# Self-attention on one core: row sums by additions on POOL, work items in two halves around the maxima, a halved item's result taken one slot later

## The chip, the cores and the metric

The kernel runs on one core of one Trainium2 chip. The metric is the device time of one execution in microseconds (us). The core has five engines with a queue each: TensorE (PE, matmuls), VectorE (DVE), ScalarE (ACT), GpSimd (POOL) and SyncE (SP, which issues DMAs). An instruction starts when those before it on its engine are done and its semaphore waits are met.

## The reference

A decoder layer: gated recurrence, cross-attention, then self-attention with a mixture of experts; the change lies in the self-attention alone. For B=4 batches of T=512 tokens, H=512, 16 heads of 32, in float32:

```python
q = (h @ wq + bq).reshape(B, S, N_HEADS, HEAD_DIM)
...
q, k = _rope(q, k)
...
scores = jnp.einsum('bqhd,bkhd->bhqk', q, k) * HEAD_DIM ** (-0.5)
causal = jnp.tril(jnp.ones((S, S), bool))
scores = jnp.where(causal[None, None], scores, jnp.finfo(scores.dtype).min)
attn = jax.nn.softmax(scores, axis=-1)
ctx = jnp.einsum('bhqk,bkhd->bqhd', attn, v).reshape(B, S, N_HEADS * HEAD_DIM)
x = x + ctx @ wo
h = _rms(x, w_ln2).reshape(B * S, H)
```

## The kernel before

`self_attention` runs 16 **steps** n = 0 to 15. Step n is batch b = n // 4 and group c = n % 4 of four heads. Each step has four **slots** kt = 0 to 3, one for each block of 128 keys; under the causal mask slot kt covers the last 512 - 128 kt queries. One slot on PE is, in order:

- `scores(n, kt)` (L1727, L1731, L1733): the scores of the four heads, keys on partitions, into four PSUM banks, with the row maximum taken off (`negm`, L1731) and the mask added.
- the slot's **early items** (`put`): projections and transposes of other steps that fill PE while ACT works, each into bank 6 or 7 in turn. An A item is the query or key projection of step n+2, a V item 128 rows of values, an O item 128 rows of the output projection (12 matmuls through L134 each). An H item transposes the normed input of the next batch (L1675), G, R and L items belong to the experts. H items are **late items**: they come behind the slot.
- `maxima(n + 1, 3 - kt)` (L1717, L1719): scores of the next step with queries on partitions, for its row maxima, into the same four PSUM banks. It waits for Exp, which empties them.
- `weighted(n, kt)`: probabilities times values (L1745), and probabilities times a block of ones (L1747), which are the sums for the softmax; each is four matmuls in float32, added up over the four slots in banks 4 and 5.

After slot 3 PE puts the T item (L1711), which turns the maxima; ACT writes them to `negm` (L1501), and the next step's scores begin.

ACT does in each slot Exp (L1529) from the four banks into `pT[:, kt % 2]`, then takes the items' results out of banks 6 and 7 (`take`; A: L1495 to `qk`, V: L1497). DVE does in each slot `maximum(n + 1, 3 - kt)` (L1616), a reduction from the four banks which frees them for the next slot's scores, then for an A item the shuffle (L1581) and the product with the sine (L1583) that the rotation needs, for an O item the two residual additions (L1593, L1595). At the end of the step it takes the reciprocal of the sums (L1648) and scales the output (L1650). POOL rotates step n+2's query and key during step n (`rotate`: L1427 waits for ACT's `qk`, L1430 for DVE's sine product), sometimes takes an inverse root (L1420), and behind the step's last scores splits the rotated pair into a high and a low part (L1444, L1447).

The `Steps` class writes out by hand which item stands in which slot. A items stand in slots 0 and 2 where c = 0 and in slots 0 and 1 elsewhere; V items of the own batch in slots 1 and 3 where c = 0, of the next batch in slots 2 and 3 where c = 3; O items of the batch before in slot 3 where c = 1 (two) and in slots 2 and 3 where c = 2. Batch 0 has no O items, the last batch no H items.

## Time and profile before

| | us |
|---|---|
| median of 3 runs | 2553.0 (2551.19 to 2557.34) |
| the profiled execution, its own time | 2558.96 |
| its span, first to last instruction | 2557.2 |
| TensorE busy in the span | 2399.1 (94%) |
| VectorE busy | 1353.7 (53%) |
| ScalarE busy | 1348.8 (53%) |
| GpSimd busy | 919.3 (36%) |

The 16 steps lie between 1407 and 1821 us of the span. In rows of a time line the first column is the start, the second how long the merged instructions took from the first start to the last end; then engine, line, operation, names (written<-read), shapes and count. In brackets stands how long the engine sat idle before the row, and what ended the idle time. Matmuls overlap, so that the time PE spends on a row is best read as the distance from its start to the start of the next. A float32 matmul with 32 rows of output shows as two records.

### The profile page before, as it was taken

The numbers are of one execution on the slowest core, as the hardware profiler recorded it, in microseconds if no ns is written. First come the engines' busy times: TensorE is split into PE (matmuls) and PEld (weight loads), VectorE is DVE, ScalarE is ACT, GpSimd is POOL, SyncE is SP. The second block draws the span as 40 slices with busy tenths as digits, with TensorE's granted clock in tenths as the row PEclk, the third lists the DMA queues.
The fourth block names the chain that finished last, engine by engine and source line by source line (L and its number), as shares of the span: only waits on it lengthen the run. The fifth ranks groups of instructions, "written<-read, shape, count | busy, mean of one in ns | idle before, by whom it ended". The sixth has DMA issues, their size and how long they took to land. (4 is left out here: it accounts for less than half of the span.)

```text
span 2557.2 us, 39125 instructions
## 1 busy us (share of the span) xinstructions
PE 2399.1 (94%) x15376; PEld 1547.3 (61%) x15376; DVE 1353.7 (53%) x2114; ACT 1348.8 (53%) x1708; POOL 919.3 (36%) x608
## 2 busy tenths in 40 slices
PE   7997899989999999999997999998899999999997
PEld 5885644444444444444333555555578899999885
DVE  5566634434344434434413556555475577776785
ACT  4221467666767777767895434433332266665221
POOL 1223744655355544655202333332034012121320
PEclk8998999999999999999999999999899999999999
DMA  5002675576547653775653300001045267775430
GB/s 181 17 1 72 192 224 126 126 197 170 141 116 209 168 153 93 180 203 143 173 124 104 111 1 1 18 18 53 34 140 170 90 228 233 243 244 186 152 113 37
DMA packets 206983, 331.46 MB, mean 130 GB/s; under 512 B 71312, under 2 KB 125840, under 8 KB 206608
## 3 DMA queue, kind: packets, MB, share of 16 engines
q1 hardware_dynamic: 188304, 252.80, 34.9%
q0 software_dynamic: 16336, 72.23, 8.6%
q10 hardware_dynamic: 2160, 3.93, 0.6%
q8 instruction: 122, 2.00, 0.3%
q14 instruction: 61, 0.50, 0.1%
HBM read 241.53 MB, written 99.42 MB: 133 GB/s over the span
## 5 line engine op out<-in xcount | busy, mean ns | idle before, releaser
L938 ACT ACTIVATE A_c_prob<-c_psum 128x1024 f32<-128x1024 f32 x832 | 787.1, 1029 | 285.9 <-PE c_psum L1188 273.0
L864 POOL TENSOR_TENSOR c_rr<-c_ms,c_half 128x32 f32<-128x32 f32 (+1 forms) x72 | 372.6, 5177 | 426.4 <-DVE c_ms L955 424.8
L1197 PE MATMUL c_psum<-A_c_prob,c_vq 128*17 128x512 f32 x3328 | 417.0, 601 | 8.3 <-DVE c_oT L1092 8.1
L134 PE MATMUL c_psum<-R_c_w,S_c_c 128*128 128x512 f32 x1248 | 313.9, 401 | 0.7 <-DVE S_c_c L966 0.5
L1188 PE MATMUL c_psum<-c_qq,c_kq 64*128 64x512 f32 x1664 | 288.3, 438 | 26.6 <-DMA c_vq<-vd 14.5
L134 PEld LDWEIGHTS c_psum<-R_c_w,S_c_c 128*128 128x128 f32 x1248 | 227.9, 189 | 121.9 <-issue 40.7
L1188 PEld LDWEIGHTS c_psum<-c_qq,c_kq 64*128 64x128 f32 x1664 | 136.9, 186 | 175.6 <-ACT A_c_prob L938 92.6
L995 DVE COPY Q_c_unit<-c_psum 128x256 f32<-128x256 f32 x89 | 37.8, 425 | 333.6 <-PE c_psum L134 333.6
L2363 PE MATMUL m_psum<-A_m_dn_hi,A_m_a 128*128 128x512 f32 (+1 forms) x628 | 204.4, 394 | 2.4 <-DVE A_m_a L2160 2.4
L134 PE MATMUL m_psum<-R_m_t,m_up_hi 128*128 128x256 f32 (+1 forms) x1104 | 200.0, 283 | 0.0
L1616 DVE TENSOR_REDUCE s_topx<-s_psum 128x4 f32<-128x2048 f32 (+1 forms) x64 | 95.5, 1493 | 172.2 <-PE s_psum L1719 167.5
L1197 PEld LDWEIGHTS c_psum<-A_c_prob,c_vq 128*17 128x17 f32 x3328 | 68.8, 96 | 189.1 <-issue 165.3
L134 PEld LDWEIGHTS m_psum<-R_m_t,m_up_hi 128*128 128x128 f32 (+1 forms) x1104 | 165.8, 179 | 2.1
L2099 ACT ACTIVATE A_m_a<-Q_m_work 128x256 fp32r<-128x256 f32 (+2 forms) x113 | 56.7, 502 | 201.4 <-DVE Q_m_work L2155 171.1
L134 PE MATMUL m_psum<-R_m_t,m_up_lo 128*128 128x256 f32 (+1 forms) x552 | 154.7, 280 | 0.0
L1529 ACT ACTIVATE A_s_pT<-s_psum 128x2048 f32<-128x2048 f32 (+1 forms) x64 | 79.5, 1242 | 125.1 <-PE s_psum L1733 124.7
L2363 PEld LDWEIGHTS m_psum<-A_m_dn_hi,A_m_a 128*128 128x128 f32 (+1 forms) x628 | 117.8, 188 | 29.0 <-DVE A_m_a L2160 3.0
L2363 PE MATMUL m_psum<-Q_m_dn_lo,A_m_a 128*128 128x512 f32 (+1 forms) x314 | 123.1, 392 | 0.0
L2092 ACT ACTIVATE Q_m_work<-m_psum 128x256 f32<-128x256 f32 (+2 forms) x113 | 51.9, 459 | 134.4 <-PE m_psum L134 133.0
L857 POOL TENSOR_TENSOR S_c_c<-Q_c_raw,S_c_c 128x512 fp32r<-128x512 f32 x89 | 118.8, 1335 | 7.1
L134 PE MATMUL m_psum<-R_g_hi,m_up_hi 128*128 128x512 f32 x264 | 105.6, 400 | 3.6 <-DVE m_up_lo L2137 3.6
L2137 DVE TENSOR_TENSOR m_up_lo<-S_up_raw,m_up_hi 128x1408 fp32r<-128x1408 f32 (+2 forms) x70 | 102.6, 1471 | 5.7 <-ACT m_up_hi L2053 3.1
(298 smaller groups left out, 4282.1 us busy)
## 6 DMA issues: line engine op xcount, KB each, us to landing
c_kq<-kd SPq DMA_DIRECT2D x248, 208.0 KB, 6.1
kd<-S_c_t SPq DMA_DIRECT2D x96, 256.0 KB
Q_c_raw<-in_ctxT SPq DMA_DIRECT2D x89, 256.0 KB
qd<-A_c_q SPq DMA_DIRECT2D x64, 256.0 KB
c_qq<-qd SPq DMA_DIRECT2D x64, 256.0 KB, 3.1
vd<-A_c_vt SPq DMA_DIRECT2D x104, 136.0 KB, 4.1
c_vq<-vd SPq DMA_DIRECT2D x31, 442.0 KB, 9.1
R_m_hs<-slots SPq DMA_DIRECT2D x23, 512.0 KB
```

Of the source, the lines that this page charges most:

```text
L134: mm = pe.matmul(out, a(c), b(c), start=first and i == 0, stop=last and i == len(terms) - 1)
L857: pool.tensor_tensor(c_lo[:, job % 2], c_raw[:, n % CB], c_hi[:, job % 2], ALU.subtract).then_inc(s_clo, 1)
L864: pool.tensor_tensor(rr[:, unit % RB, 0:n], ms[:, unit % RB, 0:n], half[:, 0:n], ALU.pow).then_inc(s_r, 1)
L938: act.activation(prob[:, t % PB, 2 * (u % 2):2 * (u % 2) + 2, :], score_banks[u % 3], ACT.Exp, scale=XD ** -0.5).then_inc(s_ex, 1)
L1188: mm = pe.matmul(score_banks[u % 3][:, s, :], kq[rows, q % 2, u % 2, kt * P:(kt + 1) * P], qq[rows, q % 2, u % 2, :], start=True, stop=True)
L1197: mm = pe.matmul(o_bank[32 * j:32 * j + VW, :], vq[:, q % 2, kt, j, :], prob[:, t % PB, j, :], start=kt == 0, stop=kt == CT - 1)
L1529: act.activation(pT[:, kt % 2, :, 0:L], psum[:, 0:HPC, 0:L], ACT.Exp, scale=SCALE).then_inc(s_ex, 1)
L1616: dve.reduce_max(topx[:, t, ::SD], psum[:, 0:HPC, 0:(t + 1) * P], AX_X).then_inc(s_top, 1)
L2092: act.activation(sig[0:rows, 0:width], gu_bank[n % 2][0][0:rows, 0:width], ACT.Sigmoid).then_inc(s_sig, 1)
L2099: act.activation(a_hi[0:rows, p % 2, i, 0:width], act_f[0:rows, 0:width], ACT.Copy).then_inc(s_ahi, 1)
L2137: dve.tensor_tensor(up_lo[:, w % 2, j, :, 0:cols(w)], up_raw[:, j, :, 0:cols(w)], up_hi[:, w % 2, j, :, 0:cols(w)], ALU.subtract).then_inc ...
L2363: mm = pe.matmul(y_bank[t], a[0:rows, p % 2, i, ts], w[0:rows, i, :], start=k == 0, stop=k == 3 * len(x.chunks) - 1)
```

## The change

The sums over keys are no longer matmuls in each slot. Exp of slot 0 writes `p_even`, those of slots 1 to 3 write `p_odd`; POOL adds each of the latter onto the matching part of `p_even` (`add`, L1460 of the changed kernel), and one set of four matmuls per step (`sums`, L1795) multiplies the added probabilities by the ones. The T item stands behind `sums` on PE. POOL's order in a step is now add 1, rotate query, add 2, rotate key, add 3, halves. Exp of slots 2 and 3 waits for the add before, since it overwrites `p_odd`. A slot's last A, V or O item is issued in two halves of six matmuls, one ahead of `maxima`, one behind `weighted` (`halved`); V item kt in slot kt stays whole. Where a halved item is held (`held`: slots 0 to 2 without late items), ACT and DVE take its result in the next slot (`taken`).

```diff
+    def halved(self, n, kt):
+        return [item for item in self.early[n][kt][-1:] if n + 1 < self.N and item.kind in "AVO" and (item.kind, item.i) != ("V", kt)]
+    def held(self, n, kt):
+        return self.halved(n, kt) if 0 <= kt < TT - 1 and not self.late[n][kt] else []
+    def taken(self, n, kt):
+        late = self.held(n, kt)
+        return self.held(n, kt - 1) + [item for item in self.early[n][kt] if item not in late]
...
-        pT = A.tile("s_pT", 0, 2, HPC, T)
+        p_even, p_odd = (A.tile(f"s_p{i}", i * HPC * T, HPC, T) for i in range(2))
+        pT = [p_even, p_odd[:, :, 0:T - P], p_odd[:, :, 0:T - 2 * P], p_odd[:, :, 0:P]]
...
+            def add(n, kt):
+                pool.wait_ge(s_pv, n * TT + 1)
+                pool.wait_ge(s_ex, n * TT + kt + 1)
+                if kt > 1:
+                    pool.wait_ge(s_add, n * (TT - 1) + kt - 1)
+                pool.tensor_tensor(pT[0][:, :, kt * P:T], pT[0][:, :, kt * P:T], pT[kt], ALU.add).then_inc(s_add, 1)
...
+            for n in range(STEPS):
+                b, c = divmod(n, KC)
+                more = n + 2 < STEPS
+                add(n, 1)
+                if c == KC - 1 and b:
+                    inverse_root("O", b - 1)
+                if more:
+                    rotate(n + 2, 0)
+                add(n, 2)
+                if more:
+                    rotate(n + 2, 1)
+                add(n, 3)
+                if c == 0 and b + 1 < B:
+                    inverse_root("H", b + 1)
+                if more:
+                    halves(n + 2)
...
-                    if n * TT + kt >= 2:
-                        act.wait_ge(s_pv, n * TT + kt - 1)
+                    if kt == 0 and n:
+                        act.wait_ge(s_sum, n)
...
+                    if kt >= 2:
+                        act.wait_ge(s_pv, n * TT + kt)
+                        act.wait_ge(s_add, n * (TT - 1) + kt - 1)
...
-                    for item in line.early[n][kt]:
+                    for item in line.taken(n, kt):
                         take(item)
...
-                dve.wait_ge(s_pv, n * TT + TT)
+                dve.wait_ge(s_sum, n + 1)
...
-                for j in range(HPC):
-                    mm = pe.matmul(sum_bank[rows[j], qs], ones[:], pT[:, kt % 2, j, 0:L], start=kt == 0, stop=True, skip_group_check=True)
-                mm.then_inc(s_pv, 1)
+            def sums(n):
+                pe.wait_ge(s_add, (n + 1) * (TT - 1))
+                for j in range(HPC):
+                    mm = pe.matmul(sum_bank[rows[j], :], ones[:], pT[0][:, j, :], start=True, stop=True)
+                mm.then_inc(s_sum, 1)
...
+                    for item in halved:
+                        put(item, 0)
                     if more:
                         if kt == 0:
                             pe.wait_ge(s_hi, 2 * n + 2)
                         pe.wait_ge(s_ex, n * TT + kt + 1)
                         maxima(n + 1, TT - 1 - kt)
                     weighted(n, kt)
+                    for item in halved:
+                        put(item, 1)
                     for item in line.late[n][kt]:
                         put(item)
+                sums(n)
                 if more:
                     put(line.turn[n + 1])
```

DVE's queue through step 4 (c = 0), from the reciprocal of step 3 to the last reduction, first before (`s_topx` rows are the maxima of step 5, the `s_turned` pairs the sine products of the two A items):

```order
L1648 RECIPROCAL s_a<-s_psum 128x512
L1650 TENSOR_TENSOR s_a<-s_psum,s_a 128x512
L1616 TENSOR_REDUCE s_topx<-s_psum 128x4
L1620 SCALAR_TENSOR_TENSOR A_s_a_15499<-s_a,s_bv,A_s_a_15498 128x512
L1581 STREAM_SHUFFLE s_turned<-s_qk 128x512
L1583 TENSOR_TENSOR s_turned<-s_turned,s_sin 128x512
L1616 TENSOR_REDUCE s_topx<-s_psum 128x4 x2
L1581 STREAM_SHUFFLE s_turned<-s_qk 128x512
L1583 TENSOR_TENSOR s_turned<-s_turned,s_sin 128x512
L1570 TENSOR_SCALAR s_ms<-s_ss 128x4
L1616 TENSOR_REDUCE s_topx<-s_psum 128x4
```

And now, the same stretch to its end, with the reciprocal of the step behind it:

```order
L1684 RECIPROCAL s_a<-s_psum 128x512
L1686 TENSOR_TENSOR s_a<-s_psum,s_a 128x512
L1652 TENSOR_REDUCE s_topx<-s_psum 128x4
L1656 SCALAR_TENSOR_TENSOR A_s_a_15500<-s_a,s_bv,A_s_a_15499 128x512
L1652 TENSOR_REDUCE s_topx<-s_psum 128x4
L1617 STREAM_SHUFFLE s_turned<-s_qk 128x512
L1619 TENSOR_TENSOR s_turned<-s_turned,s_sin 128x512
L1652 TENSOR_REDUCE s_topx<-s_psum 128x4
L1606 TENSOR_SCALAR s_ms<-s_ss 128x4
L1652 TENSOR_REDUCE s_topx<-s_psum 128x4
L1617 STREAM_SHUFFLE s_turned<-s_qk 128x512
L1619 TENSOR_TENSOR s_turned<-s_turned,s_sin 128x512
```

The first pair moved from slot 0 to slot 1, the second from ahead of the step's last reduction to behind it.

POOL's queue of one step where c = 2, before (`Q_s_qk` rows are the halves):

```order
L1427 TENSOR_TENSOR s_rot<-s_qk,s_cos 128x512
L1430 TENSOR_TENSOR s_rot<-s_rot,s_turned 128x512
L1427 TENSOR_TENSOR s_rot<-s_qk,s_cos 128x512
L1430 TENSOR_TENSOR s_rot<-s_rot,s_turned 128x512
L1444 CAST Q_s_qk_1776<-s_rot 128x512 x2
L1447 TENSOR_TENSOR Q_s_qk_1777<-s_rot,Q_s_qk_1776 128x512 x2
```

And now (`A_s_p_15497` is `p_even`, `A_s_p_15498` is `p_odd`):

```order
L1460 TENSOR_TENSOR A_s_p_15497<-A_s_p_15497,A_s_p_15498 128x4x384
L1440 TENSOR_TENSOR s_rot<-s_qk,s_cos 128x512
L1443 TENSOR_TENSOR s_rot<-s_rot,s_turned 128x512
L1460 TENSOR_TENSOR A_s_p_15497<-A_s_p_15497,A_s_p_15498 128x4x256
L1440 TENSOR_TENSOR s_rot<-s_qk,s_cos 128x512
L1443 TENSOR_TENSOR s_rot<-s_rot,s_turned 128x512
L1460 TENSOR_TENSOR A_s_p_15497<-A_s_p_15497,A_s_p_15498 128x4x128
L1450 CAST Q_s_qk_1776<-s_rot 128x512 x2
L1453 TENSOR_TENSOR Q_s_qk_1777<-s_rot,Q_s_qk_1776 128x512 x2
```

Three additions came in, and the last, on which `sums` waits, stands behind both rotations.

PE's queue in slot 3 of step 4 from the last mask matmuls of the item-free part on, before:

```order
L1717 MATMUL s_psum<-Q_s_qk_1776 128x128 x4
L1719 MATMUL s_psum<-s_neg,ident 128x128 x4
L1745 MATMUL s_psum<-A_s_pT,s_v 32x128 x4
L1747 MATMUL s_psum<-A_s_pT,s_ones 32x128 x4
L1711 MATMUL s_psum<-ident,s_topx 128x128 x4
```

And now:

```order
L1761 MATMUL s_psum<-Q_s_qk_1776 128x128 x4
L1763 MATMUL s_psum<-s_neg,ident 128x128 x4
L1789 MATMUL s_psum<-A_s_p_15498,s_v 32x128 x4
L1795 MATMUL s_psum<-A_s_p_15497,s_ones 32x512 x4
L1754 MATMUL s_psum<-ident,s_topx 128x128 x4
```

The sums of the whole step, 512 wide, stand where those of slot 3, 128 wide, stood; the ones of slots 0 to 2 are gone.

## Rows read from the trace of the kernel before

**Rows 1.** Busy time of each engine in two stretches, from Exp 0 to Exp 0

```profile
core 0: us, PE busy (x) PEld busy (x) DVE busy (x) ACT busy (x) POOL busy (x), PEclk, DMA share, GB/s
1526.24:1552.17 25.93, 23.85 (x233) 15.25 (x233) 16.15 (x19) 13.45 (x18) 11.44 (x11) 1.00 0.00 1
```

**Rows 2.** Time line of PE in step 4 (c = 0)

```profile
1505.10 0.51 PE L1727 MATMUL s_psum<-Q_s_qk 32*128 32x512 f32 x4
...
1506.51 0.71 PE L134 MATMUL s_psum<-S_s_h,R_s_hi 128*128 128x512 f32 x2
...
1509.45 0.51 PE L1717 MATMUL s_psum<-Q_s_qk 32*128 32x512 f32 x4
...
1511.11 1.04 PE L1747 MATMUL s_psum<-A_s_pT,s_ones 128*32 128x512 f32 x8
1512.68 0.45 PE L1727 MATMUL s_psum<-Q_s_qk 32*128 32x384 f32 x4 [0.53 <-DVE s_topx L1616]
...
1513.79 0.48 PE L134 MATMUL s_psum<-R_s_hi,S_s_h 128*128 128x512 f32 x1
...
1516.72 0.45 PE L1717 MATMUL s_psum<-Q_s_qk 32*128 32x384 f32 x4
...
1518.10 0.83 PE L1747 MATMUL s_psum<-A_s_pT,s_ones 128*32 128x384 f32 x8
1519.35 0.39 PE L1727 MATMUL s_psum<-Q_s_qk 32*128 32x256 f32 x4 [0.42 <-DVE s_topx L1616]
...
1525.19 0.33 PE L1727 MATMUL s_psum<-Q_s_qk 32*128 32x128 f32 x4 [0.32 <-DVE s_topx L1616]
...
1530.48 0.63 PE L1711 MATMUL s_psum<-ident,s_topx 128*128 128x128 f32 x4
```

**Rows 3.** Time line of ACT, step 4 and the start of step 5

```profile
1506.74 1.88 ACT L1529 ACTIVATE A_s_pT<-s_psum 128x2048 f32<-128x2048 f32 x1 [0.93 <-PE s_psum L1733]
...
1514.02 1.46 ACT L1529 ACTIVATE A_s_pT<-s_psum 128x1536 f32<-128x1536 f32 x1 [1.80 <-PE s_psum L1733]
...
1532.67 1.88 ACT L1529 ACTIVATE A_s_pT<-s_psum 128x2048 f32<-128x2048 f32 x1 [0.93 <-PE s_psum L1733]
```

**Rows 4.** Time line of DVE in step 4

```profile
1510.33 2.29 DVE L1616 TENSOR_REDUCE s_topx<-s_psum 128x4 f32<-128x2048 f32 x1 [1.94 <-PE s_psum L1719]
...
1525.07 0.73 DVE L1581 STREAM_SHUFFLE s_turned<-s_qk 128x512 f32<-128x512 f32 x1
1525.83 0.69 DVE L1583 TENSOR_TENSOR s_turned<-s_turned,s_sin 128x512 f32<-128x512 f32 x1
...
1529.64 0.69 DVE L1616 TENSOR_REDUCE s_topx<-s_psum 128x4 f32<-128x512 f32 x1 [3.04 <-PE s_psum L1719]
```

**Rows 5.** Groups of POOL instructions, each shape apart: busy us, mean ns

```profile
L1427 POOL TENSOR_TENSOR s_rot<-s_qk,s_cos 128x512 f32<-128x512 f32 x30 | 38.4, 1281 | 137.5 <-ACT s_qk L1495 137.5
...
L883 POOL CAST R_s_hi<-A_c_stage 128x2048 fp32r<-128x2048 f32 x2 | 3.8, 1900 | 12.8 <-DMA A_c_stage<-in_wq 12.1 <-DMA A_c_stage<-in_wv 0.6
```

**Rows 6.** Time line of POOL ahead of step 0

```profile
1405.06 4.58 POOL L1447 TENSOR_TENSOR Q_s_qk<-s_rot,Q_s_qk 128x512 fp32r<-128x512 f32 x2
```

**Rows 7.** Time line of ACT: Exp 0 of steps 2 and 3

```profile
1458.59 1.89 ACT L1529 ACTIVATE A_s_pT<-s_psum 128x2048 f32<-128x2048 f32 x1 [0.92 <-PE s_psum L1733]
...
1480.82 1.88 ACT L1529 ACTIVATE A_s_pT<-s_psum 128x2048 f32<-128x2048 f32 x1 [0.92 <-PE s_psum L1733]
```

**Rows 8.** Time line of PE: the T item at the end of step 5

```profile
1560.31 0.66 PE L1711 MATMUL s_psum<-ident,s_topx 128*128 128x128 f32 x4 [1.53 <-DVE X L1595]
```

**Rows 9.** Time line of ACT in step 15

```profile
1811.03 1.45 ACT L1529 ACTIVATE A_s_pT<-s_psum 128x1536 f32<-128x1536 f32 x1
...
1815.07 1.03 ACT L1529 ACTIVATE A_s_pT<-s_psum 128x1024 f32<-128x1024 f32 x1 [1.44 <-PE s_psum L1733]
```

**Rows 10.** Busy time by stretch behind step 15, columns as in group 1

```profile
1824.00:1828.00 4.00, 1.08 (x3) 0.92 (x4) 3.18 (x5) 1.49 (x3) 0.00 (x0) 0.78 0.00 0
1828.00:1832.00 4.00, 4.00 (x11) 3.13 (x10) 1.41 (x3) 0.00 (x0) 0.00 (x0) 0.50 0.00 0
```

**Rows 11.** Time line of PE: the first scores of step 15

```profile
1803.25 0.80 PE L1727 MATMUL s_psum<-Q_s_qk 32*128 32x512 f32 x4
```

More of the change, by code:

```diff
@@ L1359, in self_attention @@
         rr = m.sb("rr", [P, TT])
-        unused = pT[:, 1, :, T - P:T]
+        unused = p_odd[:, :, T - P:T]
         psum, bank = m.banks()
@@ L1370, in self_attention @@
         s_vs, s_qb, s_tc, s_turned, s_sin, s_rot, s_hi, s_lo = m.sem("vs", "qb", "tc", "turned", "sin", "rot", "hi", "lo")
-        s_max, s_top, s_ng, s_st, s_ex, s_pv = m.sem("max", "top", "ng", "st", "ex", "pv")
+        s_max, s_top, s_ng, s_st, s_ex, s_pv, s_add, s_sum = m.sem("max", "top", "ng", "st", "ex", "pv", "add", "sum")
         s_rec, s_a, s_ahi, s_alo, s_x1, s_x = m.sem("rec", "a", "ahi", "alo", "x1", "x")
@@ L1430, in rotate, with halves @@
                 pool.tensor_tensor(rot[:, i], rot[:, i], turned[:, i], ALU.add).then_inc(s_rot, 1)
-            pool.wait_ge(s_ld, 80)
-            for n in range(1, STEPS):
-                for i in range(2):
-                    rotate(n, i)
-                if n % KC == 2 and n // KC + 1 < B:
-                    inverse_root("H", n // KC + 1)
-                if n % KC == 1 and n // KC >= 2:
-                    inverse_root("O", n // KC - 2)
+            def halves(n):
                 if n >= 2:
@@ L1447, in _ @@
                     pool.tensor_tensor(qk_lo[:, n % 2, i], rot[:, i], qk_hi[:, n % 2, i], ALU.subtract).then_inc(s_lo, 1)
-            for b in (B - 2, B - 1):
-                inverse_root("O", b)
+            def add(n, kt):
[4 more added lines that the diff above has]
+                pool.tensor_tensor(pT[0][:, :, kt * P:T], pT[0][:, :, kt * P:T], pT[kt], ALU.add).then_inc(s_add, 1)
+            pool.wait_ge(s_ld, 80)
+            for i in range(2):
+                rotate(1, i)
+            halves(1)
+            for n in range(STEPS):
[14 more added lines that the diff above has]
+                    halves(n + 2)
+            inverse_root("O", B - 1)
         @block.scalar
@@ L1638, in _ @@
                         low_output(n - 1)
-                    for item in line.early[n][kt] + line.late[n][kt]:
+                    for item in line.taken(n, kt) + line.late[n][kt]:
                         take(item)
@@ L1662, in _, with put, product @@
             rows = [slice(SD * j, SD * j + SD) for j in range(HPC)]
-            def put(item):
+            def put(item, part=None):
                 dst = bank_of(item)
-                if item.old:
+                if item.old and part != 1:
                     pe.wait_ge(emptied[item.old.kind], item.old.nth)
                 i, n = item.i, item.n
+                k0, k1 = {None: (0, KC), 0: (0, KC // 2), 1: (KC // 2, KC)}[part]
+                def product(lhs_hi, lhs_lo, rhs_hi, rhs_lo):
+                    return product3(pe, dst, lambda k: lhs_hi(k0 + k), lambda k: lhs_lo(k0 + k), lambda k: rhs_hi(k0 + k), lambda k: rhs_lo(k0 + k),
+                                    k1 - k0, first=k0 == 0, last=k1 == KC)
                 b, c = divmod(n, KC)
@@ L1679, in put @@
                         pe.wait_ge(s_hlo, b * KC)
-                    mm = product3(pe, dst, lambda k: w_hi[i][:, k, fs], lambda k: w_lo[i][:, k, fs], *h, KC)
+                    mm = product(lambda k: w_hi[i][:, k, fs], lambda k: w_lo[i][:, k, fs], *h)
                 if item.kind == "V":
@@ L1683, in put @@
                         pe.wait_ge(s_hlo, n * KC)
-                    mm = product3(pe, dst, lambda k: h_hi[:, k, ts], lambda k: h_lo[:, k, ts], lambda k: w_hi[2][:, k, :], lambda k: w_lo[2][:, k, :], KC)
+                    mm = product(lambda k: h_hi[:, k, ts], lambda k: h_lo[:, k, ts], lambda k: w_hi[2][:, k, :], lambda k: w_lo[2][:, k, :])
                 if item.kind == "O":
@@ L1688, in put @@
                     at = lambda k: (n * KC + k) % RING
-                    mm = product3(pe, dst, lambda k: a_hi[:, at(k), ts], lambda k: a_lo[:, at(k), ts], lambda k: w_hi[3][:, k, :], lambda k: w_lo[3][:, k, :], KC)
+                    mm = product(lambda k: a_hi[:, at(k), ts], lambda k: a_lo[:, at(k), ts], lambda k: w_hi[3][:, k, :], lambda k: w_lo[3][:, k, :])
                 if item.kind == "G":
@@ L1711, in put @@
                         mm = pe.transpose(dst[:, t * P:(t + 1) * P], topx[:, t, :], ident[:])
-                mm.then_inc(s_put, 1)
+                if part != 0:
+                    mm.then_inc(s_put, 1)
             def maxima(n, t):
@@ L1766, in _ @@
                     scores(n, kt)
-                    for item in line.early[n][kt]:
+                    early = line.early[n][kt]
+                    halved = line.halved(n, kt)
+                    for item in early[:len(early) - len(halved)]:
                         put(item)
+                    for item in halved:
+                        put(item, 0)
                     if more:
```

9 lines of the change are left out of this document (5 added, 4 removed).

## The prediction, made before the changed kernel ran

> **What bounds the kernel now.** I first looked at busy time over one step. Of 25.93 us PE is busy 23.85 and POOL 11.44, and the granted clock is 1.00, the 2.4 GHz level [rows 1]. So PE sets the pace here and POOL has 14 us free. The time line of PE shows how a slot is spent. The reader is to see two things in it. First, PE hardly waits: only 0.53, 0.42 and 0.32 us ahead of the scores of slots 1 to 3, each time for DVE's reduction [rows 2]. Second, behind PE's own work runs a second chain through the four PSUM banks that is nearly as long: scores, Exp, maxima, reduction, next scores.
>
> For slot 0 that chain is 1.64 us from scores to Exp (1505.10 to 1506.74), Exp 1.88, 0.05 to hand over, 0.88 from maxima to reduction (1509.45 to 1510.33), reduction 2.29, 0.06 to hand over: 6.80 us. The slot takes 7.58 (1505.10 to 1512.68), because the item of 2.94 us keeps PE beyond Exp's end [rows 2 to 4].
>
> **What the change takes out, by slot.** Issue times are distances between starts. The sums of slot 0 cost PE about 0.89 us, those of slot 1 0.67; by width I take 0.45 and 0.25 for slots 2 and 3. That is 2.26 per step, of which 0.89 is paid once again in `sums`. Halving the item moves 1.47 us behind `weighted`, where it covers the reduction.
> - Slot 0: PE would need 3.57 to Exp's end, 1.66 for maxima and weighted (1509.45 to 1511.11) and 1.47 for the second half, 6.70; the bank chain is 6.80. From 7.58 to 6.80: 0.78 gained.
> - Slot 1: scores to Exp is 1.34 (1512.68 to 1514.02), Exp 1.46, so maxima begin at 2.85; then 1.38 (1516.72 to 1518.10) and 1.47 give 5.70, from 6.67: 0.97 gained.
> - Slot 2 in the same way: about 4.94 from 5.84, 0.90 gained.
>
> Slots 0 to 2 thus give 2.65 us wherever each has a halved item. Exp loses its cover in slot 0 (0.65 us of PE waiting), and this is already in these numbers.
>
> **What the change adds: the chain on POOL.** `sums`, and behind it T and the next scores, wait for add 3, and add 3 is behind add 1, two rotations and add 2. No row shows an addition of this shape. Product with the cosine, two inputs in SBUF, is 1.281 us for 512 elements [rows 5]. The adds cover 1536, 1024 and 512 elements: by proportion 3.84, 2.56 and 1.28, together 7.7 us. From below I bound them by the one-input CAST, 1.900 for 2048 elements [rows 5]: 2.85 us in all. From above by the pair of subtractions that ran while DVE read two SBUF inputs: 4.58 us instead of 2.56, 1.8 times as much [rows 6], 13.8 us in all. I take 7.7, since the nearest row has the same operation and type.
>
> The Trainium skill, GPSIMD Engine Reference, section 3.1, gives 4497 ns for a float32 addition of 2048 elements. Estimated from that page the adds would be 3.4, 2.2 and 1.1 us, 0.9 less per step, and the sum below would come out some 6 us lower, at about 2552.
>
> Counted from the start of scores 1: Exp 1 ends at 2.80, add 1 at 6.7. Each rotation is 2.57 (two instructions of 1.28), so the rest is 2.57 + 2.56 + 2.57 + 1.28, and add 3 ends at 15.7. Exp 2 and Exp 3 wait for the adds before them by 0.2 us at most, which is hidden under the first half of the item. PE reaches the place of `sums` at 5.70 + 4.94 + 4.57 = 15.2 where slot 3 has a halved item (0.81 scores, 2 x 1.47 item, 0.59 maxima, 0.23 weighted). Then 0.95 for `sums`, 0.56 for T, 6.80 for slot 0: the new period is 15.7 + 8.3 = 24.0. Now by kind of step:
>
> - Steps 3, 6, 10 (c = 3 of batch 0, c = 2 with O items): 24.0 from 25.93 (distance of Exp 0 to Exp 0, as 1506.74 to 1532.67 [rows 3]): -1.9 each, **-5.8**.
> - Steps 7 and 11: an inverse root of 1.0 us stands in POOL's chain: -0.9 each, **-1.8**.
> - Step 2 has no items in slots 2 and 3 and took 22.23 [rows 7]. It becomes 24.0, since POOL's chain does not care: **+1.7**. Step 1 likewise **+0.5**.
> - Steps 5, 9, 13: slot 3 holds two O items, so add 3 is long done when `sums` comes. T ended its wait for DVE's O item at 1560.31 [rows 8]; the halved item lets DVE begin 1.5 us sooner. With 0.78 in slot 0, 0.6 in slots 1 and 2 (H items fill there) and 1.2 in slot 3: -2.6 each, **-7.8**. Step 14: 2.26 - 0.95, **-1.3**.
> - Steps 0, 4, 8, 12 (c = 0). Here the second A item is in slot 2, is held, and DVE's shuffle and sine product now stand behind the step's last reduction. The whole V item of slot 3 is still ahead of those maxima, so the reduction ends 5.14 us after scores 3 (1525.19 to 1529.64, and 0.69) [rows 2, 4]. Then shuffle 0.73 and product 0.69 [rows 4], POOL's rotation sum 1.29, add 3 1.28, `sums` 0.95 and hand-overs 0.15: T starts at 10.2 instead of 5.29 (1525.19 to 1530.48 [rows 2]). That is 4.9 lost against 2.65 gained: +2.25 each, **+9.0**.
> - Step 15 has no cover: Exp 2 waits for add 1, at 1811.03 + 1.45 + 3.94 = 1816.4 instead of 1815.07 [rows 9]; step 15's last add and full-width sums lie bare on the way to the tail. Add 2 makes up for part: **+1.9**.
>
> Sum: -3.8 us. So the work saved is paid back by the wait for add 3.
>
> **And the clock.** In the four steps with c = 0 PE stands idle from the end of weighted, about 4.9 after scores 3, to 9.3: 4.4 us, more than any wait inside the steps today. The trace shows what followed a long wait: in 1824 to 1828 PE was busy 1.08 us of 4, and in the 4 us after it the granted clock was 0.50, the 1.2 GHz level [rows 10]. After the 1.53 us wait [rows 8] it stayed at 1.00. Scores at a lowered clock took 0.80 against 0.51 for the same four matmuls [rows 2, 11]. Sums, T and scores together are 0.89 + 0.56 + 1.41 = 2.86 us on the path, and between 0.57 and 1.0 times as much again is 1.6 to 2.9; I take 2.3, four times: **+9.2**. The Trainium skill, TensorE: Matmul & The Clock Gate, part 1, says that the engine is throttled to half its clock when it idles and is released by activity; by that rule the trace agrees (0.50 behind the wait), and it speaks against this change.
>
> Sum with the clock: +5.4 us. The profiled execution's own time is 2558.96 (span 2557.2, 1.8 around it) and would become 2564.4; it is 6 above the median of the runs, 2553.0, which would become **2558**.
>
> **Edits costed at nothing.** The later take of A and V results: banks 6 and 7 alternate, and the item before is taken in the slot after, ahead of its bank's next use. DVE's reciprocal (3.36 of work behind `sums` instead of behind slot 3) has to be ready by weighted 0, about 5.5 us after T starts; it is, with under 1 us to spare. If that cover is gone it is a wait in weighted 0 of what is missing. The halves of step n+2 end 5 us ahead of their use. No DMA is moved.
>
> **The rivals.**
> - The clock holds (free of the +9.2): 2553 - 4 = **2549**. For it: 1.5 us waits left it at 1.00 [rows 8]. Against: the wait here is three times as long.
> - POOL is slower than by proportion (the other side: slower). Place: add 1 to add 3, in front of `sums`. DVE's sine products read two SBUF inputs inside that chain, and such an overlap stretched a pair from 2.56 to 4.58 [rows 6]; four pieces per partition may cost too. At 25% more on the adds the seven steps 1, 2, 3, 6, 7, 10, 11 lose 1.9 each, the four with c = 0 0.3, the tail 1.5: 16 us, with the clock **2574**, without it 2565. It decides (beyond 0.3%, 7.7 us) from 5% on if the clock falls.
> - POOL is much cheaper, towards the CAST, and the clock holds: then PE's own work bounds. Steps 3, 6, 10 gain 0.5 more, 7 and 11 1.5, 1 and 2 about 2, c = 0 0.5: 10 us more than -4, **2539**.
>
> **How the numbers follow.** Forecast 2558: 0.42. Clock holds, 2549: 0.25. POOL slower: 0.20. POOL cheaper: 0.13. 0.3% is 7.7 us, about what a measurement of this kernel tells from no change. Of the forecast's spread (2553 to 2563) a quarter is beyond +7.7, of the second case a sixth beyond -7.7. Slower: 0.20 + 0.11 = 0.31. Faster: 0.13 + 0.04 = 0.17. Same: 0.52. Leaving out the far half of each outer case gives 2544 to 2571.
>
> **What would show it.** Adds of 3.8, 2.6 and 1.3 us; POOL busy about 19 of a 24 us step; PE idle about 4.4 us ahead of `sums` in steps 0, 4, 8 and 12 and 0.5 to 3 in the others but 5, 9, 13; a period of 28.2 (more with the clock) for c = 0 and 24.0 for steps 3, 6, 10; the clock below 1.00 behind the waits of c = 0. I am wrong if the adds are off by more than 10%, if the clock holds, or if DVE's reciprocal turns up as a wait.

## The result, and the profile after

The changed kernel took 2567.8 us (median of 8 runs, 2564.4 to 2578.6); the kernel before took 2558.3 in its 8 runs of the same measurement (2551.2 to 2562.5). The ratio is 1.0049, with a 95% interval from 1.0035 to 1.0064: slower by 0.49%, 12.5 us of 2558 (9 to 16). A second measurement of the same kernel, below, gave 1.0045. The forecast was +5.4 us (2558), with a chance of 0.52 for a change within 0.3%, 0.31 for slower, and a range of 2544 to 2571. The sign came out as foreseen and the time lies in the slow part of the range, but the loss is 2.3 times the size forecast, and the case that came was not the one I held likeliest.

The profiled execution of the changed kernel took 2578.62 us (span 2576.9), 11 above the median of its runs; the one of before was also above its median. So I compare distances between Exps here, not spans. Busy time over step 4 (c = 0), in three stretches of 4 us around its end, and over step 6 (c = 2); columns as in [rows 1]:

```profile
core 0: us, PE busy (x) PEld busy (x) DVE busy (x) ACT busy (x) POOL busy (x), PEclk, DMA share, GB/s
1517.26:1548.56 31.30, 26.24 (x205) 15.59 (x205) 16.50 (x16) 11.19 (x19) 17.52 (x13) 0.90 0.00 1
1540.00:1544.00 4.00, 1.01 (x8) 0.20 (x8) 0.32 (x1) 0.00 (x0) 3.54 (x4) 0.78 0.00 0
1544.00:1548.00 4.00, 4.00 (x30) 1.98 (x23) 3.00 (x1) 0.60 (x1) 3.52 (x4) 0.50 0.00 0
1548.00:1552.00 4.00, 3.66 (x26) 2.21 (x26) 1.59 (x3) 3.44 (x4) 0.00 (x0) 0.87 0.02 4
1576.98:1601.75 24.77, 24.06 (x205) 14.46 (x205) 16.75 (x18) 8.78 (x13) 16.30 (x11) 1.00 0.01 2
```

Step 4 took 31.30 us where it took 25.93 [rows 3]; step 6, which also took 25.93, took 24.77. In step 4 the granted clock is 0.90 on the whole, and 0.50, the 1.2 GHz level, from 1544 to 1548.

The stretch of [rows 1] is as long as step 4, but it doesn't run from Exp 0 to Exp 0: those are at 1506.74 and 1532.67 [rows 3]. Over step 4 itself, before the change, the row is

```profile
1506.74:1532.67 25.93, 24.42 (x229) 15.60 (x229) 13.20 (x15) 11.41 (x19) 9.73 (x9) 1.00 0.01 2
```

so POOL was busy 9.73 us of it, and not 11.44. In step 6 it was 8.81.

The time line of PE at the end of step 4 shows the wait itself. Here the sums of the step, then T, then scores 0 of step 5 follow:

```profile
1538.40 0.42 PE L1789 MATMUL s_psum<-A_s_p,s_v 128*32 128x128 f32 x8 [0.18 <-ACT s_v L1530]
1542.99 1.93 PE L1795 MATMUL s_psum<-A_s_p,s_ones 128*32 128x512 f32 x8 [4.16 <-POOL A_s_p L1460]
1544.86 1.12 PE L1754 MATMUL s_psum<-ident,s_topx 128*128 128x128 f32 x4
1545.90 0.80 PE L1771 MATMUL s_psum<-Q_s_qk 32*128 32x512 f32 x4
```

PE stands idle for 4.16 us ahead of `sums`, released by POOL's addition (L1460). Behind the wait T takes 1.12 us instead of 0.66 and the first scores 0.80 instead of 0.51 [rows 2, 8]. What POOL waited for is on the time lines of DVE and POOL:

```profile
1538.26 0.69 DVE L1652 TENSOR_REDUCE s_topx<-s_psum 128x4 f32<-128x512 f32 x1 [3.74 <-PE s_psum L1763]
...
1538.87 0.72 DVE L1617 STREAM_SHUFFLE s_turned<-s_qk 128x512 f32<-128x512 f32 x1
1539.62 0.69 DVE L1619 TENSOR_TENSOR s_turned<-s_turned,s_sin 128x512 f32<-128x512 f32 x1
```

```profile
1536.11 1.29 POOL L1440 TENSOR_TENSOR s_rot<-s_qk,s_cos 128x512 f32<-128x512 f32 x1 [1.62 <-ACT s_qk L1528]
1540.46 1.26 POOL L1443 TENSOR_TENSOR s_rot<-s_rot,s_turned 128x512 f32<-128x512 f32 x1 [3.06 <-DVE s_turned L1619]
1541.68 1.26 POOL L1460 TENSOR_TENSOR A_s_p<-A_s_p,A_s_p 128x512 f32<-128x512 f32 x1
```

The chain reads: last reduction, shuffle, product with the sine, POOL's rotation sum, add 3, `sums`. POOL was idle for 3.06 us in the middle of it. It isn't short of time; its queue holds add 3 behind a rotation that waits for DVE.

The additions by shape, and the product with the cosine, from 1407 to 1850 [rows 5]:

```profile
L1460 POOL TENSOR_TENSOR A_s_p<-A_s_p,A_s_p 128x1536 f32<-128x1536 f32 x16 | 55.7, 3483 | 152.1 <-ACT A_s_p L1565 152.1
L1440 POOL TENSOR_TENSOR s_rot<-s_qk,s_cos 128x512 f32<-128x512 f32 x28 | 44.5, 1591 | 6.6 <-ACT s_qk L1528 6.6
...
L1460 POOL TENSOR_TENSOR A_s_p<-A_s_p,A_s_p 128x1024 f32<-128x1024 f32 x16 | 38.0, 2375 | 1.6 <-ACT A_s_p L1565 1.6
...
L1460 POOL TENSOR_TENSOR A_s_p<-A_s_p,A_s_p 128x512 f32<-128x512 f32 x16 | 20.4, 1277 | 6.0 <-ACT A_s_p L1565 6.0
```

The additions cost 3.48, 2.38 and 1.28 us, the first two less than I had taken. The product with the cosine rose from 1281 ns [rows 5] to 1591 on average.

By kind of step, the distance from Exp 0 to Exp 0, against before. The steps measured are those of a second profiled execution of the changed kernel (r1_changed below), in which the clock held in step 1:

| steps | forecast, all together | measured |
|---|---|---|
| 0, 4, 8, 12 (c = 0) | +18.2 (9.0 wait, 9.2 clock) | +17.6 |
| 3, 6, 10 | -5.8 | -3.5 |
| 7, 11 | -1.8 | -0.5 |
| 5, 9, 13 | -7.8 | -3.2 |
| 1 and 2 | +2.2 | +5.3 |
| 14 | -1.3 | -2.3 |
| sum of the 15 steps | +3.7 | +13.4 |

The first profiled execution gives +18.8 for the sum: its step 1 took 26.91 us where this one's took 24.55, and each of its steps 0, 4, 8 about 1 us more.

### The profile page after: what moved, and what is told of

The parts are those of the page before. It is cut to its first block and busy times, and to the rows that moved or that the text cites. A ratio compares the mean times of both kernels' runs of the same rounds, so it can differ in the third digit from the quotient of the medians.

```text
span 2576.9 us, 38446 instructions
## 1 busy us (share of the span) xinstructions
PE 2404.2 (93%) x14992; PEld 1536.7 (60%) x14992; DVE 1369.6 (53%) x2114; ACT 1346.2 (52%) x1708; POOL 1040.9 (40%) x656
## 5 line engine op out<-in xcount | busy, mean ns | idle before, releaser
L1460 POOL TENSOR_TENSOR A_s_p<-A_s_p,A_s_p 128x1536 f32<-128x1536 f32 (+2 forms) x48 | 114.2, 2378 | 159.8 <-ACT A_s_p L1565 159.8
L1565 ACT ACTIVATE A_s_p<-s_psum 128x2048 f32<-128x2048 f32 (+1 forms) x64 | 79.4, 1240 | 153.1 <-PE s_psum L1777 136.3
L2067 POOL DMA_INDIRECT S_up_raw<-in_up,m_up_row x46 | 44.4, 964 | 164.1 <-DVE m_up_lo L2192 163.8
```

Of the source, the lines that this page charges most:

```text
L1460: pool.tensor_tensor(pT[0][:, :, kt * P:T], pT[0][:, :, kt * P:T], pT[kt], ALU.add).then_inc(s_add, 1)
L1565: act.activation(pT[kt], psum[:, 0:HPC, 0:L], ACT.Exp, scale=SCALE).then_inc(s_ex, 1)
```

## The experiments

Theory A was that the loss sits in the four steps with c = 0 and comes from add 3's place behind the late rotation. Theory B was that it is POOL's extra work as such. Theory C was that the gain of halving is small, whoever makes the sums. All ratios are to the kernel before in runs on the same chip.

**Add 3 ahead of the second rotation.**

```
                 add(n, 2)
+                add(n, 3)
                 if more:
                     rotate(n + 2, 1)
-                add(n, 3)
```

> POOL's order is add 1, rotate query, add 2, add 3, rotate key. Theory A (the loss is the wait of the sums for add 3, long only because add 3 stands behind the key's rotation): in steps with c = 0 add 3 ends about 3 us after the last scores start, ahead of PE, so the 4.2 us wait and the lowered clock behind it go; about 6.8 us less in each of steps 0, 4, 8 and 12, and 3 to 4 less in steps 1 and 2: 30 us below the changed kernel, near 2537 to 2545, 0.5 to 0.8% faster than before. Theory B (the additions load POOL too much wherever they stand, or PE loses by the halved items): the order moves work only, under 8 us less, near 2560 to 2567.

Measured: 2539.9 us, ratio 0.9944 (0.9931 to 0.9958), 14 us faster than before and, by the two ratios, about 27 faster than the changed kernel. Nothing but the order of one queue differs. The c = 0 steps take 24.57 instead of 30.3, which is 23 of the 27 us. The first fence is from the list of PE's waits in the changed kernel (us in total, times, longest); the second has Exp 0 of steps 4, 5 and 6 on ACT with add 3 first:

```profile
PE s_psum L1795 <- POOL A_s_p L1460: 22.9, 9, 4.2
```

```profile
1501.62 1.88 ACT L1565 ACTIVATE A_s_p<-s_psum 128x2048 f32<-128x2048 f32 x1 [0.93 <-PE s_psum L1777]
1526.19 1.88 ACT L1565 ACTIVATE A_s_p<-s_psum 128x2048 f32<-128x2048 f32 x1 [0.93 <-PE s_psum L1777]
1554.68 1.88 ACT L1565 ACTIVATE A_s_p<-s_psum 128x2048 f32<-128x2048 f32 x1 [0.93 <-PE s_psum L1777]
```

With add 3 first, `sums` waited 1.4 us in all, in two places, instead of 22.9 in nine; from Exp 0 of step 4 to that of step 5 it is 24.57 us. POOL does as much work as before the edit (1039.2 us busy against 1040.9). Theory B had under 8 us less, and falls by this.

**The second A item of c = 0 taken in its own slot.** This removes the same wait from the other side: DVE gets its shuffle and product done before the last reduction, and POOL's order stays as in the changed kernel.

```
     def held(self, n, kt):
-        return self.halved(n, kt) if 0 <= kt < TT - 1 and not self.late[n][kt] else []
+        return self.halved(n, kt) if 0 <= kt < TT - 1 and not self.late[n][kt] and (n % KC, kt) != (0, 2) else []
```

> The changed kernel, but the second A item of the steps with c = 0 is taken by ACT and DVE in its own slot 2 (still in two halves); POOL's order stays. Theory A (the wait of c = 0 comes from the sine product behind the step's last reduction): the product is ready 4 us earlier, add 3 ends about when PE is done, c = 0 falls from 31.3 to 25 or 26 us, 20 us below the changed kernel: 2542 to 2550. Theory B (it is add 3 behind any second rotation, held or not): under 6 us gained.

Measured: 2549.0 us, 0.9978 (0.9967 to 0.9988). The c = 0 steps take 25.2 us, and the waits ahead of `sums` come to 7.9 us in all instead of 22.9. So four takes, each moved by one slot, turn a kernel slower by 0.45% into one faster by 0.22%. This and the edit before confirm theory A twice, by independent edits.

**Additions left out.** POOL only signals where each addition stood, and `sums` multiplies the cosine table, so the softmax is divided by sums that are not its own; everything else is computed.

```
-                pool.tensor_tensor(pT[0][:, :, kt * P:T], pT[0][:, :, kt * P:T], pT[kt], ALU.add).then_inc(s_add, 1)
+                pool.sem_inc(s_add, 1)
```

> Leaves the additions out: POOL only signals, and the sums' four matmuls read a constant tile, so that the softmax is divided by wrong sums. Everything else as in the changed kernel, POOL's order with its waits too. Theory A (the place in POOL's queue, not POOL's load): the signal of add 3 still comes behind the key's rotation, so c = 0 keeps 29 to 30 us; the other steps lose what the additions cost them, steps 1 and 2 about 2 to 4 us each; 8 to 12 us below the changed kernel. Theory B (POOL's load): c = 0 falls to 25 us as well, 35 us below.

Measured: 2550.5 us, 0.9985 (0.9976 to 0.9994). Even with 120 us of POOL's work gone (920.2 busy against 1040.4), the c = 0 steps still take 28.1 to 28.4 us, 2.2 to 2.5 more than in the kernel before. That is under the 29 to 30 I expected, and the kernel came out 14.8 us below the changed one on the same chip, not 8 to 12. PE still waits ahead of its sums (here L1796), for a signal that stands behind the rotation in POOL's queue:

```profile
1530.60 1.07 PE L1796 MATMUL s_psum<-s_cos,s_ones 128*32 128x512 f32 x8 [1.87 <-POOLq L1460]
```

```profile
1530.36 1.27 POOL L1443 TENSOR_TENSOR s_rot<-s_rot,s_turned 128x512 f32<-128x512 f32 x1 [3.06 <-DVE s_turned L1619]
```

The rows show one thing more. `sums` began at 1530.60, 0.24 us into the rotation's last instruction and 1.03 ahead of its end (1531.63), and so it did in all four c = 0 steps: the bare signal waited for the instruction ahead of it to start, not to end. So this kernel leaves out more than the additions, and its wait is too short. As an estimate, a signal at the rotation's end would make it 1.87 + 1.03 = 2.9 us, and add 3 itself (1.26) brings that to the 4.16 measured. Most of the wait is made by the place in the queue; the additions lengthen it. A kernel with free additions in this order would be slower than one with real additions in the better order (2550.5 against 2539.9, on two chips whose kernel before took 2553.8 and 2553.5).

**Sums on PE, halves and late takes kept.** All of the change but the additions: PE makes the sums of each slot again, POOL has its old order.

```
-        pT = [p_even, p_odd[:, :, 0:T - P], p_odd[:, :, 0:T - 2 * P], p_odd[:, :, 0:P]]
+        pT = A.tile("s_pT", 0, 2, HPC, T)
...
+            for n in range(1, STEPS):
+                for i in range(2):
+                    rotate(n, i)
```

> Items in halves and results taken late as in the changed kernel, but the sums as matmuls in each slot and POOL's queue as before the change. Theory A: with the additions gone nothing waits for POOL; the halves gain 0.3 to 0.4 us in slots 1 and 2 less 0.2 us that each halved item costs PE in hand-overs: within 5 us of before. Theory B (the halves themselves cost the time): as slow as the changed kernel, 2565 or more.

Measured: 2566.7 us, 1.0049 (1.0035 to 1.0062), outside what I expected. The c = 0 steps took 25.97 and the steps 3, 6, 10 25.7 to 26.5, no gain. By its number it is what theory B gave, so the run has to be read step by step. The list of PE's waits tells why the undisturbed steps gain nothing: those for the maxima (scores behind DVE's reduction) fell from 16.6 us to 1.1, but those for Exp (maxima behind ACT) rose from 8.3 to 19.7, and new ones came up for POOL's halves (3.7) and for DVE's scaled output (3.2, from 0.3). With PE's own sums in place a halved item only trades one wait for the others. Most of the loss (9.0 of 13.7 us over the steps) lies in two steps and has, as I read the trace, another source, a fault of my kernel rather than of the idea. In steps 7 and 11 (31.17 and 29.72 us) the late take delays a rotation, and the inverse root is behind it in POOL's old order. ACT's normalise stands ahead of Exp 3 and begins 0.11 us behind the root's end (the trace names no releaser for it):

```profile
1607.98 1.28 POOL L1442 TENSOR_TENSOR s_rot<-s_rot,s_turned 128x512 f32<-128x512 f32 x1 [1.91 <-DVE s_turned L1595]
1609.22 1.02 POOL L1432 TENSOR_TENSOR s_rr<-s_ms,s_half 128x4 f32<-128x4 f32 x1
```

```profile
1610.35 1.33 ACT L1485 ACTIVATE A_s_xs<-A_s_xs,s_rr 128x512 f32<-128x512 f32 x2 [5.62 <-issue]
```

It is the same fault of order as that of add 3, with another operation behind the late rotation. The changed kernel has the root right behind add 1 and doesn't suffer from it. No run with the root moved tests this reading. The run therefore tells what halves do in the undisturbed steps (nothing), and not what the part costs as a whole.

**Items whole, additions on POOL**, once in the changed kernel's order and once with add 3 first.

```
     def halved(self, n, kt):
-        return [item for item in self.early[n][kt][-1:] if n + 1 < self.N and item.kind in "AVO" and (item.kind, item.i) != ("V", kt)]
+        return []
```

> Sums by additions on POOL as in the changed kernel, but each item whole and taken in its own slot. Slots 0 to 2 then go back to 7.6, 6.7 and 5.8 us, since the sums that left PE lay under DVE's reduction. Theory A: A1 of c = 0 is taken in slot 2, so the sine product is ready in slot 3 and the wait of 4.2 us shrinks to 1 to 2; each step pays sums (0.95) and a wait for add 3 in the steps without O or V items at its end: 5 to 15 us slower than before. Theory B: the wait for add 3 stays as long as in the changed kernel and nothing is gained in the slots: 30 us slower than before.

> Items whole and taken at once, add 3 ahead of the key's rotation: neither halves nor any long wait. Slots stay at 7.6, 6.7, 5.8 us, each step pays the sums at its end, 0.95 less the 0.25 of slot 3's: about 0.3 us slower per full step, 1 to 2 in steps 1 and 2: 0.1 to 0.4% slower than before, 2555 to 2562. If additions gain by themselves, it is faster than before.

Measured: 2562.7 us, 1.0040 (1.0026 to 1.0053), and 2561.0, 1.0026 (1.0017 to 1.0036). Both lie where I expected them. With whole items nothing is held, so add 3 is seldom late (`sums` waits 2.9 us in three places in the first, 1.1 in two in the second), and its place matters little. The full steps take 26.2 to 26.5 us, 0.3 to 0.6 more than before. The waits for the maxima in the first of these kernels, and below them those of the kernel before:

```profile
PE s_psum L1771 <- DVE s_topx L1652: 41.5, 38, 1.4
```

```profile
PE s_psum L1727 <- DVE s_topx L1616: 16.6, 38, 0.6
```

The same 38 places, and 25 us more. The sums of slots 0 to 2 are gone from PE, but they had stood under DVE's reduction, so that PE now waits out most of what it saved, and pays 1.0 us for the sums of the step on top. Halves alone gain nothing, additions alone lose, and both together with add 3 first gain 1.1 to 1.4 us in each full step (24.57 for c = 0, 24.7 for steps 3, 6, 10, 24.8 for steps 7 and 11). Each part needs the other: one takes PE's work out from under the reduction, and the other puts the item there.

**The wait filled with PE work**, to price the clock: in c = 0 steps 16 matmuls into a bank that is free go ahead of `sums`; their results are not used.

```
+                if n % KC == 0:
+                    item = line.turn[n + 1]
+                    pe.wait_ge(emptied[item.old.kind], item.old.nth)
+                    for k in range(16):
+                        pe.matmul(bank_of(item), w_hi[0][:, k % KC, 0:P], h_hi[:, k % KC, :], start=True, stop=True)
```

> The changed kernel, and in the four steps with c = 0 PE runs 16 matmuls of 512 columns into the bank of the T item, which overwrites them, ahead of the sums (extra work, no result changed). Theory A, its clock part: the wait stays about as long in sum (3.7 us of matmuls, then the rest of 4.2) but the clock stays at 1.00, so sums, T and scores take 2.9 us and not 5: 2 to 2.5 us less per step, 8 to 10 us below the changed kernel. Theory B (the clock costs nothing here): no gain, or up to 1 us more per step where the matmuls outlast the wait.

Measured: 2567.8 us, 1.0055 (1.0041 to 1.0069). In the steps it was meant for, it did what was expected. The granted clock stayed at 1.00, and behind a rest wait of 0.39 us the sums took 1.06 us instead of 1.93:

```profile
1532.61 3.92 PE L1835 MATMUL s_psum<-S_s_h,R_s_hi 128*128 128x512 f32 x16
1536.91 1.06 PE L1795 MATMUL s_psum<-A_s_p,s_ones 128*32 128x512 f32 x8 [0.39 <-POOL A_s_p L1460]
```

```profile
1536.00:1540.00 4.00, 3.61 (x36) 1.68 (x35) 1.95 (x1) 0.60 (x1) 4.00 (x5) 1.00 0.02 4
```

The c = 0 steps took 29.0 us each, against 30.3 in the one profiled execution of the changed kernel and 30.8 to 31.3 in the other: the fall of the clock costs between 1.3 and 2.3 us a time. But the whole kernel gained nothing. Part of the reason is in its step 9, next to the same step of r1_changed, the second run of the changed kernel:

```profile
1648.08:1677.77 29.69, 27.52 (x221) 17.37 (x221) 18.81 (x22) 12.49 (x17) 17.82 (x13) 0.94 0.00 1
```

```profile
1649.20:1677.62 28.42, 26.05 (x221) 16.45 (x221) 18.29 (x22) 12.39 (x16) 16.46 (x11) 1.00 0.00 1
```

The same 221 matmuls, the same waits of up to 1.11 us, and the clock fell to 0.94 in the one, to hold at 1.00 in the other: 1.27 us. Steps 1 and 13 lost 1.3 each in the same way against r1_changed (step 1 was slower still, 26.91, in the first profile of the changed kernel). The kernel with the A item taken in its own slot shows the same in step 9 (29.76 us at a clock of 0.94), again without a wait over 1.11 us. Why the clock falls in such a step in one kernel and not in another isn't settled by these runs.

**The changed kernel again**, on the same chip as three of the others:

> The changed kernel once more, beside the others on this chip: 0.4 to 0.6% slower than before. Its steps with c = 0 take 31 us where the clock falls behind the wait and 29 where it does not; if the clock is what spreads its times, this profile shows fewer of the one than the first.

Measured: 2565.3 us, 1.0045 (1.0032 to 1.0058). The wait at 1535.47 is 4.16 us again, to the hundredth, but the clock recovers sooner (0.94 over step 4, where it was 0.90), and the step takes 30.29 us instead of 31.30. The length of the waits repeats; what the clock makes of them doesn't quite.

**The sparse steps filled**, and the better version once more, as its neighbour. Steps 1 and 2 have no items in some slots. On top of add 3 first:

```
+                    if (n, kt) in ((1, 3), (2, 2), (2, 3)):
+                        item = line.turn[n + 1]
+                        pe.wait_ge(emptied[item.old.kind], item.old.nth)
+                        for k in range(5 if kt == 2 else 4):
+                            pe.matmul(bank_of(item), w_hi[0][:, k % KC, 0:P], w_hi[0][:, k % KC, :], start=True, stop=True)
```

> Add 3 ahead of the key's rotation, and in slot 3 of step 1 and slots 2 and 3 of step 2, which have no early item, PE runs 4 or 5 matmuls of 512 columns into the T item's bank while it waits for Exp (extra work, overwritten by T). With add 3 first the clock fell behind these slots alone, in steps 1 and 2 (0.57 and 0.54 in the trace), where sums and T took 2.8 us and not 1.6. Theory (that is the price of a lowered clock): it stays at 1.00, 1 to 2.5 us less in each of the two steps, 2 to 5 us faster than with add 3 first alone, about 0.993 of before. Rival: the matmuls outlast Exp and give it back; no change.

> The kernel with add 3 ahead of the key's rotation once more, beside the filled one: 0.5 to 0.65% faster than before.

Measured: 2539.4 us, 0.9949 (0.9935 to 0.9963), and 2537.7, 0.9946 (0.9933 to 0.9959). The filling gained nothing, against what I expected. Steps 1 and 2 took 25.05 and 22.56 us with it, 23.52 and 23.54 without it, and 26.54 and 24.02 in the first run of the same kernel: they vary by 3 us between two executions of one program. The clock differs with them: over step 1 it was 0.93, 1.00 and 0.87 in the same order, over step 2 1.00, 0.93 and 0.86. The stretch 1448 to 1452, the end of step 1 in the first run and the change to step 2 in the second, has a granted clock of 0.57 and of 1.00:

```profile
1448.00:1452.00 4.00, 3.80 (x24) 1.73 (x28) 2.11 (x2) 0.60 (x1) 3.92 (x6) 0.57 0.01 4
```

```profile
1448.00:1452.00 4.00, 4.00 (x37) 2.34 (x30) 3.08 (x1) 1.60 (x2) 3.92 (x5) 1.00 0.02 4
```

So matmuls in the gaps of step 2 may have kept the clock up there, but step 1 lost it even so, and one profile of each can't tell this from the spread of 3 us. The repeat does confirm the version with add 3 first, 0.54 to 0.56% faster than before; among the kernels here only the filled one (0.51%) is as fast.

## Why the forecast came out short of the loss

**Right: what the step at c = 0 costs.** The chain of reduction, shuffle, product, rotation sum, add 3 and sums was foreseen piece by piece, at 4.4 us of idle PE (measured 4.16). So was the fall of the clock behind it. Steps of 28.2 us without the clock's part and 30.5 with it were forecast; 29.0 was measured with the clock held, 30.3 and 31.3 with it falling. Two experiments remove the loss, one in POOL's queue and one in DVE's. That the table has +17.6 next to +18.2 is partly luck. With the clock held these four steps lose 12.4 us, where I had 9.0; the fall of the clock adds 5.2 (8.5 in the first profile), where I had 9.2. The 0.8 per step that I missed is the term of the next paragraph.

**Luck in the sign.** Without the clock my sum was a gain of 3.8 us (its terms add up to 3.6; I had slipped by 0.2), so the slower kernel was forecast by the clock's +9.2 alone. The run with the filled wait kept the clock at 1.00 in all four steps and was slower by 0.55% all the same; even without the 1.3 us that it lost in each of steps 1, 9 and 13 it would lie above 2560, so the rival "the clock holds, 2549" finds no support. Nor does the one with cheap additions (2539): with no additions at all, and the signal early, the kernel took 2550.5. Both counted on the gain of halving, which is smaller than I took.

**Wrong: what halving gains where nothing waits.** I took 6.80, 5.70, 4.94 and 4.57 us for the four slots of a full step. The time line of PE in step 6, at the points from which they are read:

```profile
1575.35 0.50 PE L1771 MATMUL s_psum<-Q_s_qk 32*128 32x512 f32 x4
...
1579.01 0.51 PE L1761 MATMUL s_psum<-Q_s_qk 32*128 32x512 f32 x4 [0.61 <-ACT A_s_p L1565]
...
1579.78 1.07 PE L1789 MATMUL s_psum<-A_s_p,s_v 128*32 128x512 f32 x8
1580.77 0.74 PE L134 MATMUL s_psum<-S_s_h,R_s_hi 128*128 128x512 f32 x2
...
1582.36 0.45 PE L1771 MATMUL s_psum<-Q_s_qk 32*128 32x384 f32 x4
...
1588.28 0.39 PE L1771 MATMUL s_psum<-Q_s_qk 32*128 32x256 f32 x4
...
1593.54 0.33 PE L1771 MATMUL s_psum<-Q_s_qk 32*128 32x128 f32 x4
...
1598.53 1.07 PE L1795 MATMUL s_psum<-A_s_p,s_ones 128*32 128x512 f32 x8
```

The slots took 7.01, 5.92, 5.26 and 4.99, together 1.17 more. The term at fault is the half item. I took 1.47, half of 2.94; the second half in slot 0 takes 1.59 (1580.77 to 1582.36), and the time from weighted to it is 0.99 (1579.78 to 1580.77), where I had 0.89. An item cut in two starts and ends twice, and my sum had nothing for the second time. So PE needs 16.17 us from scores 1 to `sums` (with some 0.15 behind Exp 1), where I had put 15.2, and the period is 24.77, not 24.0. The same term takes 0.75 from slots 0 to 2 of the c = 0 steps (18.19 us in step 4, where I had 17.44). Steps 7 and 11 gained 0.2 us each instead of 0.9: there `sums` did wait, 0.9 us, for POOL's chain with the root in it, which is longer than I had it for a reason given below.

This also decides where the bound lies. I had POOL's chain end after 15.7 us; it ended at 1598.48, 16.1 us after scores 1, and `sums` began at 1598.53 with no wait recorded. PE and POOL end together here. The experiment with add 3 first shows that PE's own work is the bound: with POOL's part out of the way early, step 6 still took 24.68 us.

**Wrong: steps 5, 9 and 13.** The gain was put at 2.6 each and was 1.4 in steps 5 and 9, 0.3 in step 13. The time line of the changed step 5 has the wait for DVE's O item gone, as foreseen (1.53 us [rows 8]). But part of that was needed to pay for the full-width sums, and slot 0 gained 0.57 (from Exp 0 to scores 1, 5.94 before and 5.37 after) instead of 0.78, slots 1 and 2 together 0.26 instead of 0.6, slot 3 to T 0.60 (9.63 and 9.03) instead of 1.2. In slot 0 the missing 0.21 is the half item's again; for the rest I had carried the gains of full steps over to slots that hold other items. In step 13 the clock was 0.94 besides, where it had been 1.00 before; with add 3 first it was 1.00 and the step took 26.38. The better result of step 14 (-2.3 for -1.3) goes with the clock too, 0.94 before and 1.00 now.

**Wrong: steps 1 and 2.** I let step 2 be bound by POOL's chain at 24.0; it took 26.3 in one execution and 26.0 in the other. In r1_changed `sums` waited there for 1.92 us and then ran at the lower clock (1.94 us instead of 1.06). I had asked of four steps only what the clock would do. A step with little PE work behind a wait was the other place to ask it; with the additions left out, steps 1 and 2 took 22.9 and 22.8.

**Right for a wrong reason: POOL's chain.** By proportion the adds were to cost 7.7 us; they cost 7.1. That is within the 10% that I had set as a sign, and no wait of PE for DVE's reciprocal turned up either. POOL busy 19 us a step was wrong, though: it is 16.3 in step 6, because I had added the 7.7 to the 11.44 of [rows 1], a stretch that isn't a step. The Trainium skill, GPSIMD Engine Reference, section 3.1, gave the estimates of 3.4, 2.2 and 1.1 us, nearer than mine for the two large ones and below the measured 1.28 for the small one. The product with the cosine, in turn, costs more than [rows 5] has, when DVE makes its product with the sine at the same time. POOL and DVE in step 6:

```profile
1588.73 1.74 POOL L1440 TENSOR_TENSOR s_rot<-s_qk,s_cos 128x512 f32<-128x512 f32 x1
...
1591.79 2.39 POOL L1460 TENSOR_TENSOR A_s_p<-A_s_p,A_s_p 128x1024 f32<-128x1024 f32 x1
1594.13 1.74 POOL L1440 TENSOR_TENSOR s_rot<-s_qk,s_cos 128x512 f32<-128x512 f32 x1
```

```profile
1588.48 0.84 DVE L1619 TENSOR_TENSOR s_turned<-s_turned,s_sin 128x512 f32<-128x512 f32 x1
...
1593.41 1.31 DVE L1619 TENSOR_TENSOR s_turned<-s_turned,s_sin 128x512 f32<-128x512 f32 x1
```

Twice 0.46 more on POOL more than makes up for the 0.6 of the cheaper additions. The 1.74 us aren't a slower product but a wait for a turn. DVE's second product started at 1593.41 while add 2 ran until 1594.18, and ended at 1594.72, 0.54 behind it; POOL's product, shown from 1594.13, ended 1.15 behind that. The last section has all such meetings. [rows 6] fits too: DVE's difference of two SBUF inputs of 2048 elements ran from 1405.07 to 1408.51, and POOL's pair ended 1.13 behind it. So its 4.58 us are 2.56 and the wait for one long DVE instruction, and no factor of 1.8 to be applied to the additions. The rival in which POOL is cheaper and the clock holds (2539) thus didn't come; the rival in which it is slower than by proportion (2574) was right that the two engines meet, and wrong about the operation that pays and about the price. The sum by that page's figures, about 2552, would have been further off, since the cheaper adds come with the dearer product.

**What stays open.** The price of the clock for the whole kernel. By the profiles it is 1.3 to 2.3 us for each fall, but the kernel that kept the clock up in four steps was no faster than the changed one, and steps 1, 2, 9 and 13 show falls that come and go between kernels and between executions. The tail isn't settled either. Of step 15 itself the trace shows 2.5 us more, from Exp 0 (1805.91 before, 1823.76 now) to DVE's reciprocal, with Exp 2 waiting 2.60 us for add 1 as foreseen:

```profile
1821.14 3.36 DVE L1648 RECIPROCAL s_a<-s_psum 128x512 f32<-128x512 f32 x1 [0.82 <-PE s_psum L1747]
```

```profile
1841.54 3.36 DVE L1684 RECIPROCAL s_a<-s_psum 128x512 f32<-128x512 f32 x1 [4.46 <-PE s_psum L1795]
```

But what lies outside the 15 steps differs by 8 us between two profiled executions of the changed kernel, 4.6 of it ahead of step 0, so that the +1.9 for step 15 and the tail together can't be checked. The excess of steps 1 and 2 over the forecast, 3 us, is therefore only in part put down to a cause.

## What to carry to other kernels

When work moves to an engine with time to spare, look for what stands ahead of it in that engine's queue and what that waits for. Here POOL had over 8 us free in each step, and its result came 4 us late because one instruction ahead of it waited for DVE; exchanging two calls was worth 27 us, where leaving the additions out altogether was worth 15, some 4 of that only because the signal then came early. Two edits that each gain nothing can gain together, if one frees the time that the other fills, so they have to be priced as a pair. And a piece of work cut in two is to be priced from a row of such a piece, not as half of the whole.
